# One PSUM bank for z instead of two, four instead of three for the ring of short-lived tiles, and another job order, in a causal attention and LoRA kernel

## What is computed

```
q, k, v  = W_Q xn, W_K xn, W_V xn                   # 16 heads, 128 wide
scores   = q k^T with the causal mask
z        = softmax(scores / sqrt(128)) v            # per head
s        = W_O z_flat                               # 2048 x 256
g        = silu(W_base xn + b_base + 2 * LoRA of the expert that the router picks)
out      = x + s * g
```

## Time and profile before

| What | Value |
|---|---|
| Median of 3 runs | 1423.0 us (1422.2 to 1423.47) |
| The profiled execution, its own time | 1423.18 us |
| Its span, from first to last instruction | 1421.4 us |
| PE busy | 1386.3 us (98%) |
| DVE, ACT, POOL busy | 1208.4, 1089.7, 850.2 us |
| Start, up to the first scores of the attention | 48.7 us |
| One pair of heads, from 555.6 us on | 166.0 us |

### The profile page before, as it was taken

How to read it: one execution, slowest core, us unless ns; L and a number is a source line. 1 busy time by engine, 2 the same in 40 slices (tenths; PEclk the granted TensorE clock), 3 DMA queues, 4 the chain that set the end, 5 groups by cost and what they waited for, 6 DMA issues and landing times.

```text
span 1421.4 us, 22882 instructions
## 1 busy us (share of the span) xinstructions
PE 1386.3 (98%) x7532; PEld 1169.3 (82%) x7532; DVE 1208.4 (85%) x2605; ACT 1089.7 (77%) x2260; POOL 850.2 (60%) x688
## 2 busy tenths in 40 slices
PE   5899999999999999999999999999999999999996
PEld 4688888888888888888888888888888888888775
DVE  6688998889898988889988898989888899888964
ACT  2578886888778787788868887787877888688851
POOL 3265675557666575666755576665756667555850
PEclk9799999999999999999999999999999999999998
DMA  2110001000100000100010001001011000100002
GB/s 81 31 31 16 14 10 46 8 16 16 31 23 9 23 16 23 30 16 12 13 45 9 16 16 31 24 8 23 14 25 31 16 10 14 36 15 16 16 31 89
DMA packets 30070, 33.73 MB, mean 24 GB/s; under 512 B 11008, under 2 KB 17664, under 8 KB 29952
## 3 DMA queue, kind: packets, MB, share of 16 engines
q1 hardware_dynamic: 29952, 32.26, 9.1%
HBM read 30.02 MB, written 2.23 MB: 23 GB/s over the span
## 4 chain that ended last, share of the span: by engine, by line
PE 94%; DVE 3%; DMA 1%; ACT 1%; issue 1%; SPq 0%; DVEq 0%; ACTq 0%
PE ps L295 27%; PE ps L297 26%; PE ps L296 26%; PE ps L749 9%; PE ps L784 2%; PE ps L761 1%; DVE p_lo L579 1%; PE ps L812 1%; DVE partmax L593 1%; PE ps L702 0%; DMA acc<-x_dram 0%; DVE acc L571 0%; PE ps L718 0%; DVE stats L549 0%; DMA spread<-max_dram 0%
## 5 line engine op out<-in xcount | busy, mean ns | idle before, releaser
L448 POOL TENSOR_TENSOR colsum<-colsum,probs 128x512 f32<-128x512 f32 (+3 forms) x512 | 661.8, 1293 | 207.4 <-ACT probs L526 167.9
L579 DVE TENSOR_TENSOR p_lo<-probs,p_hi 128x512 fp32r<-128x512 f32 (+3 forms) x640 | 537.5, 848 | 13.7 <-ACT p_hi L527 13.6
L526 ACT ACTIVATE probs<-ps 128x512 f32<-128x512 f32 (+3 forms) x640 | 346.1, 541 | 145.1 <-PE ps L297 83.8
L503 ACT ACTIVATE ps<-maxrow 128x512 f32<-128x512 f32 (+3 forms) x640 | 356.2, 557 | 0.0
L527 ACT ACTIVATE p_hi<-ps 128x512 fp32r<-128x512 f32 (+3 forms) x640 | 345.7, 540 | 0.0
L593 DVE TENSOR_REDUCE partmax<-ps 128x1 f32<-128x512 f32 x384 | 256.5, 681 | 3.0 <-PE ps L749 0.3
L295 PE MATMUL ps<-p_hi,v_hi 128*128 128x512 f32 (+3 forms) x640 | 239.4, 374 | 1.4 <-DVE p_lo L579 0.9
L295 PE MATMUL ps<-qT_hi,kT_hi 128*128 128x512 f32 (+3 forms) x640 | 236.3, 369 | 3.6 <-ACT ps L503 3.6
L749 PE MATMUL ps<-kT_hi,qT_hi 128*128 128x512 f32 (+3 forms) x640 | 233.9, 388 | 1.7 <-DVE qT_lo L587 1.0
L297 PE MATMUL ps<-p_hi,v_lo 128*128 128x512 f32 (+3 forms) x640 | 233.2, 364 | 0.0
L296 PE MATMUL ps<-qT_lo,kT_hi 128*128 128x512 f32 (+3 forms) x640 | 233.0, 364 | 0.0
(11 more groups left out here) (108 smaller groups left out, 2232.7 us busy)
## 6 DMA issues: line engine op xcount, KB each, us to landing
spread<-max_dram SPq DMA_DIRECT2D x64, 256.0 KB, 3.8
wraw<-wqk_dram SPq DMA_DIRECT2D x16, 256.0 KB, 4.2
acc<-x_dram SPq DMA_DIRECT2D x4, 512.0 KB, 6.8
wraw<-wv_dram SPq DMA_DIRECT2D x8, 256.0 KB, 4.8
wraw<-wo_dram SPq DMA_DIRECT2D x8, 256.0 KB, 3.3
probs<-x_dram SPq DMA_DIRECT2D x4, 512.0 KB, 4.5
out_dram<-acc SPq DMA_DIRECT2D x4, 512.0 KB, 2.9
max_dram<-rowmax SPq DMA_DIRECT2D x64, 2.0 KB, 1.4
```

The source lines that it names most:

```text
L448: nc.gpsimd.tensor_tensor(total[:, c0:], total[:, c0:], tile[:, c0:], ALU.add)\
L503: nc.scalar.activation(st[job.n % SCORE_BANKS][:, c0:], maxrow[:, job.g, c0:], ACT.Copy)\
L526: nc.scalar.activation(probs[:, k, c0:], src, ACT.Exp, scale=SCALE).then_inc(probs_ready, 1)
L579: nc.vector.tensor_tensor(p_lo[:, k, c0:], probs[:, k, c0:], f32(p_hi[:, k, c0:]), ALU.subtract)\
```

## The change

`AUX_BANKS` goes from 3 to 4. The bank comes from z, which keeps one bank (3); the ring has banks 4 to 7. Two waits on PE are new: the first value matmul of every group but the first waits until `z_lo` of the group before is made, and `Base`, whose four banks now hold the only bank of z, waits for the last `z_lo`. `SCHEDULE` is another string with the same jobs.

```
-AUX_BANKS = 3
+AUX_BANKS = 4
...
 SCHEDULE = (
-    "w V10 Pk02 V00 w M0202 Pk03 V01 w z7 | s7 | Pq03 | o70 M0222 v | v o71 M0311 | v M0212 S0 | M0232 v M0313 "
+    "Pk02 V11 V01 V00 w Pk03 w M0202 w z7 | M0222 s7 | Pq03 o70 | v | M0311 M0333 v | o71 v S0 v | M0212 M0232 Z0 "
...
-        zb = [ps[:, SCORE_BANKS + k, :] for k in range(2)]
-        aux = [ps[:, SCORE_BANKS + 2 + k, :] for k in range(AUX_BANKS)]
+        zb = ps[:, SCORE_BANKS, :]
+        aux = [ps[:, SCORE_BANKS + 1 + k, :] for k in range(AUX_BANKS)]
...
-                    nc.scalar.activation(z_hi[:, :], zb[job.gi % 2], ACT.Copy).then_inc(z_hi_ready, 1)
+                    nc.scalar.activation(z_hi[:, :], zb, ACT.Copy).then_inc(z_hi_ready, 1)
...
-                    dst = zb[gi % 2][:, c0:]
+                    if job.kt == 0 and gi:
+                        pe.wait_ge(z_lo_ready, gi)
+                    dst = zb[:, c0:]
...
                 elif isinstance(job, Base):
                     pe.wait_ge(ffn_w_ready, DC + 2)
                     pe.wait_ge(hi_ready, PAIRS * TILES)
+                    pe.wait_ge(z_lo_ready, PAIRS * GROUPS)
```

More of the change, by code:

```diff
@@ L614, in _ @@
                     dve.wait_ge(z_hi_ready, job.gi + 1)
-                    nc.vector.tensor_tensor(z_lo[:, :], zb[job.gi % 2], f32(z_hi[:, :]), ALU.subtract)\
+                    nc.vector.tensor_tensor(z_lo[:, :], zb, f32(z_hi[:, :]), ALU.subtract)\
                       .then_inc(z_lo_ready, 1)
```

## The result

The changed kernel takes 1443.6 us in the median of four runs, against 1423.0 us (1422.2 to 1423.5) before: a ratio of 1.0145, 95% interval 1.0093 to 1.0198. The four runs fall into two pairs: 1438.2 and 1438.4 us with a mean granted clock of 0.989, and 1448.8 and 1448.9 us with 0.981 and 0.980.

What follows compares the result with a forecast made beforehand. PE, busy for 98% of the span, was taken as the bound. Eight pairs (1.85 of waits less 0.6 us each) +10.0, last pair +1.0, end +1.5 and start -0.85 gave +11.7 us: 1434.7 us, range 1422.5 to 1445.

Steps and rivals of the forecast that it cites:

- The bound and the pair: PE bounds the kernel and pays new waits in full, eight times: +1.25 us a pair, 166.5 to 167.9 us.
- The hand-overs of z: Waits in us: even block 3 to odd 0 1.05, odd 1-2 0.35, odd 2-3 0.2, even 0-1 0.15, odd 0-1 0.1.
- the first: Even head block 3 to odd head block 0: PE waits 1.05 us a pair for z_lo (0.92 to 1.17).
- even block 0 to 1: Even head: z_lo stands on DVE behind sums, a p_lo and two row maxima; PE waits 0.15 us (0 to 0.3).
- Room on ACT and DVE: Behind a waiting value the delay does not grow, as ACT and DVE have 30 and 20 us to spare a pair.
- The ring: Fourth bank removes PE's short waits for DVE to free a bank: gain 0.6 us a pair (0 to 1.0).
- Start and end: Start: a fourth transpose job fits into PE's pause, -0.85 us; end: `Base` waits for z_lo, +1.5 us.
- The last pair: Without a following pair's row maxima and projections, less work covers the waits: +1.0 us (0 to 3) more.
- The end ... +1.5 us: `Base` waits for the last z_lo before the last stage, with nothing to hide it: +1.5 us.
- That row maxima would run freely: Rival: fourth bank also removes 31 ns over 448 row maxima, 13.9 us, so faster, 1418 us; chance 0.08.
- That the ring pays for all: Rival: only the first place waits, 7.4 us, and all 8.0 us of short stalls go: 1423 us; chance 0.12.
- That nothing is covered: Rival: ACT or DVE late at every hand-over, 64 times 1.35 us lost: about 1510 us; chance 0.04.

Runs made afterwards that it cites:

- a run of its own: Changed kernel with last value, split and one row maximum of even block 3 one score tile earlier: 1430.4 us in the median of eight, ratio 1.007.
- four places: Changed kernel with the order mended before the first values of even block 1 and odd blocks 0, 2 and 3: 1440.4 us, ratio 1.014.
- all places mended: Changed kernel with z in bank 7, so no wait at the end, and the order mended at all four waiting places: 1438.5 us, ratio 1.011.
- the order alone: Kernel before with the new schedule, three banks in the ring and two for z: 1494.3 us, ratio 1.049.
- the second profile of the changed kernel: Changed kernel run again unchanged: three runs of 1435.6 to 1438.1 us, three of 1447.1 to 1448.1; the profiled one is of the longer kind.
- the banks alone: Changed kernel with the old job order, each z split right behind its group's last value: 1506.5 us, ratio 1.059.
- the run without any wait for z: Changed kernel with z's split reading a constant SBUF tile and both waits for z_lo left out: 1443.0 us, ratio 1.014.

## Why the prediction was right, and where it was not

**The bound and the pair.** Right. New waits of PE were paid in full, eight times: a pair takes +1.56 us against a forecast of +1.25, in the range of 166.5 to 167.9 us.

**The hand-overs of z.** Forecast 1.05, 0.35, 0.2, 0.15 and 0.1, together 1.85 us a pair. Measured 0.97, 0.49, 0.18, 0.22 and none: 1.86. Counting PE's work between last and first value against the chain on ACT and DVE gave the places and nearly the sizes; that the sums agree to 0.01 is luck. Only the first is proved by a run of its own, in which 0.76 us a pair came back. At even block 0 to 1 the reason was another than the one given: z_lo does not queue on DVE there, which stands idle for 0.38 us ahead of it, waiting for z_hi.

**Room on ACT and DVE.** "The delay does not grow", since ACT and DVE have 30 and 20 us to spare in a pair. Spare time in the mean was the wrong measure: in the runs with four places and with all places mended the waits for z went and came back as waits for DVE. And the sum had no term for what the new order itself costs on DVE: a p_lo is late in odd block 3, 0.49 us a pair. That is not a delay grown from a hand-over, since the order alone, without any wait for z, shows it as well.

**The ring.** Forecast 0.6 us a pair (0 to 1.0); what is left over from the other terms, 1.86 + 0.49 - 1.56, is 0.8. Some 0.36 of it is no gain of the ring but the wait for p_lo of the earlier trace rows, which the new order no longer has at this place (by the starts, 0.25 ahead of the value and 0.11 behind it):

```profile
743.84 0.19 PEld L295 LDWEIGHTS ps<-p_hi,v_hi 128*128 128x128 f32 x1 [0.20 <-DVE p_lo L579]
```

That leaves some 0.4 for old against new order with the bank that each was made for, an estimate from a remainder. As a statement on the bank the term says nothing: in the new order it carries 7.2 us a pair. The waits of the old trace priced a bank that the old order had been laid out to do without.

**Start and end.** The transposes come in runs of 16 and the rest, as foreseen, and the first score tile starts at 47.77 in place of 48.74 us: -0.97 against -0.85. One profile alone would not show it, since the ten with four banks start it at 46.57 to 48.50 and the four with three at 48.11 to 48.74; the means lie 1.0 us apart. The last pair from its first score to its last value takes 163.71 us against 160.33, +3.4 where 1.25 and 1.0 were forecast; in the second profile of the changed kernel it is 162.15, +1.8. The other 1.6 go with the clock, which fell for a moment in the first (the rows at 1361 us in the last section). The end took +1.67 against +1.5.

**The sum.** -0.97, 7 x 1.56, +3.4 and +1.7 are +15.0 us of span in the profiled execution, against +11.7. The forecast of 1434.7 us missed its 1438.2 by 3.5.

**The step that failed most** is "The end ... +1.5 us". The wait has that size, but a stall of PE was costed only by its length. In half of the executions of the changed kernel (5 of 10) it also takes the clock down for some 30 us and costs 12.7 us more, so the median of four lies at 1443.6 between two levels, near the upper bound of 1445, and the longer runs above it. That it lies inside the range is luck: no execution took that time, and a third long one among the four would have put the median above the range.

**The rivals.** That row maxima would run freely shows in part: those of 512 columns last 414 ns in the mean where it was 423, 9 of the 31 ns and so at most 4 us, far from enough. That the ring pays for all failed by the terms above. That nothing is covered is what the banks alone show in the old order: 9.3 us a pair, 74 us over eight pairs, where the rival had said 86 us.

**Open.** What the waits at the three smaller places would cost by themselves was not settled: the run without any wait for z also made DVE slower. Why the clock falls in some executions and not in others under the same wait is not shown either.

## What to carry to other kernels

An order of work and a set of buffers that were fitted to each other can't be priced edit by edit: run each half alone before believing a term, and expect the halves to be far worse than the whole. The mean idle time of a helper engine is no room at the place where a wait moves; look at its queue there, and after a mend look where the wait went. A stall of TensorE ahead of a new stage should be costed twice, once by its length and once by what a lower clock behind it would take if it comes: 10 to 13 us here, in 13 of 36 executions.

## What the runs showed of the hardware

An idle stretch of 1.5 us before the last stage brought the granted clock from 1.00 to 0.50 for some 30 us of almost full work on PE, in 4 of 12 executions of a kernel that differs from the one before by this wait alone. (The count is by the mean granted clock; the one that was profiled shows the stretch.) In the profiled execution of the changed kernel an idle stretch of 1.85 us in the last pair was followed by the same for a moment, 3.72 of 4.00 us busy at a mean clock of 0.57; in the second profile the clock stayed at 1.00 there.

```profile
1361.28 0.77 PE L295 MATMUL ps<-p_hi,v_hi 128*128 128x512 f32 x1 [1.85 <-DVE z_lo L615]
```

```profile
1361.00:1365.00 4.00, 3.72 (x10) 3.00 (x11) 2.40 (x3) 1.66 (x4) 1.36 (x2) 0.57 0.00 0
```

Length alone does not decide. The profile of the banks alone has 40 idle stretches of 1.38 to 1.61 us in its eight pairs, and the clock fell behind two of them, for 3.4 us each. The first row is a pair with five such stretches, the second one of the two falls:

```profile
625.00:800.20 175.20, 166.77 (x914) 140.41 (x913) 147.60 (x313) 133.91 (x281) 101.80 (x83) 1.00 0.08 19
1199.84:1203.26 3.42, 3.40 (x9) 2.84 (x10) 1.60 (x4) 0.47 (x1) 0.00 (x0) 0.50 0.03 5
```
